# First layer's attention weights: the fifth block of a pair goes to the matrix engine unsplit, in single precision

## What is computed

```
q = (norm(x) @ Wq).reshape(b, s, 32, 16);  k, v = split(norm(x) @ Wkv)    # one k and v of 16 columns for all 32 heads
scores = q k^T / 4 + slope_h * (key position - query position), causal
out = softmax(scores) @ v;  x = x + norm(out @ Wo)
```

## Time and profile before

| | us |
|---|---|
| median of the timed runs | 2204.15 |
| time of the profiled execution | 2197.44 |
| span of its trace | 2195.3 |
| steps with the 64 pairs, about | 100 to 586 |
| PE busy over the span | 2057.3 |
| DVE busy over the span | 1755.9 |
| POOL busy over the span | 937.6 |

### The profile page before, as it was taken

One profiled execution on the slowest core, in us unless ns is written; L12 is line 12 of the kernel. 1 busy time (PEld: TensorE's weight loads), 2 busy tenths in 40 slices (PEclk: granted clock), 3 DMA queues, 4 the chain that ended last, 5 costly groups with the idle time before them and its releaser, 6 DMA issues. The chain is left out here.

```text
span 2195.3 us, 48564 instructions
## 1 busy us (share of the span) xinstructions
PE 2057.3 (94%) x18563; PEld 1244.2 (57%) x18563; DVE 1755.9 (80%) x3692; ACT 1389.0 (63%) x3037; POOL 937.6 (43%) x902
## 2 busy tenths in 40 slices
PE   8788989898868999999999999999999999888998
PEld 3466666566434556666566666666666666534443
DVE  5799998998766787878878788777877887977665
ACT  3466665666456777777777777767777776661221
POOL 0278787879743223333333332333323323253221
PEclk9999999999889999999999999999999999999999
DMA  6110101101122463454345445344344444420001
GB/s 241 47 36 17 55 17 47 36 18 41 44 96 55 87 102 70 78 101 87 67 92 90 73 89 92 66 97 91 62 96 86 73 83 83 98 71 29 29 20 39
DMA packets 390214, 153.81 MB, mean 70 GB/s; under 512 B 358544, under 2 KB 369424, under 8 KB 387936
## 3 DMA queue, kind: packets, MB, share of 16 engines
q1 hardware_dynamic: 389984, 150.71, 31.6%
HBM read 48.69 MB, written 11.53 MB: 27 GB/s over the span
## 5 line engine op out<-in xcount | busy, mean ns | idle before, releaser
L1899 POOL TENSOR_TENSOR q_in_sbuf<-q_in_sbuf,sinq 128x512 f32<-128x512 f32 x128 | 162.5, 1270 | 718.0 <-ACT q_in_sbuf L2031 598.1
L2043 ACT ACTIVATE xp<-xp,nm 128x128 f32<-128x128 f32 (+3 forms) x512 | 281.3, 550 | 199.0 <-DVE nm L2126 199.0
L1925 PE MATMUL bank<-xT_hi,weights_and_hi 128*128 128x512 f16 x1280 | 382.5, 381 | 5.3 <-PEq L103 3.2
L872 ACT ACTIVATE weights_and_hi<-bank,unit 128x512 f32<-128x512 f32 x320 | 213.2, 686 | 166.4 <-PE bank L671 160.5
L2008 ACT ACTIVATE probs_hi<-xp,rl 128x128 f16<-128x128 f32 (+3 forms) x512 | 245.1, 550 | 67.3 <-DVE rl L2146 64.4
L2095 DVE SCALAR_TENSOR_TENSOR probs_lo<-xp,rl,probs_hi 128x128 f16<-128x128 f32 (+3 forms) x512 | 282.3, 611 | 0.0
L2103 DVE TENSOR_TENSOR q1T_lo<-qf,q1T_hi 128x512 f16<-128x512 f32 x128 | 88.4, 690 | 220.6 <-ACT q1T_hi L2022 220.6
L2126 DVE CUSTOM_DVE_ANT_0 xp<-bank,mask,cs 128x128 f32<-128x128 f32 (+3 forms) x512 | 250.2, 544 | 0.0
L1925 PE MATMUL bank<-xT_lo,weights_and_hi 128*128 128x512 f16 x640 | 243.6, 381 | 0.0
L564 POOL CAST weights_and_hi<-weights_and_hi 128x1024 f16<-128x1024 f32 (+1 forms) x192 | 187.7, 996 | 104.0 <-ACT weights_and_hi L872 103.7
L1925 PE MATMUL bank<-p1T_hi,v_hi 128*128 128x128 f16 x1280 | 221.4, 219 | 2.6 <-DMA p1T_lo<-probs_lo 2.6
(11 more groups left out here) (311 smaller groups left out, 5472.3 us busy)
## 6 DMA issues: line engine op xcount, KB each, us to landing
weights_and_hi<-in_wq SPq DMA_DIRECT2D x8, 1024.0 KB, 5.8
raw_o<-in_wo SPq DMA_DIRECT2D x8, 1024.0 KB, 6.1
x_front<-in_x SPq DMA_DIRECT2D x5, 1024.0 KB, 6.1
q_stack<-q_hi SPq DMA_DIRECT2D x64, 64.0 KB, 2.6
wup<-in_wup SPq DMA_DIRECT2D x3, 1024.0 KB, 11.9
fused_scratch<-weights_and_hi SPq DMA_DIRECT2D x12, 256.0 KB, 2.6
xb<-in_x SPq DMA_DIRECT2D x3, 1024.0 KB, 5.4
x_scratch<-xb SPq DMA_DIRECT2D x3, 1024.0 KB, 4.8
```

Of the source, the lines that this page charges most:

```text
L872: act.activation(px[:, p % 2, i, :], bank_of(("x", p, i))[:, :], ACT.Exp, scale=unit[:, 0:1]).then_inc(s_ed, 1)
L1899: pool.tensor_tensor(qs[:, i % 2, :], qs[:, i % 2, :], rope["sink" if u[0] == "k" else "sinq"][:, :], ALU.mult).then_inc(s_rot, 1)
L1925: ins = pe.matmul(out, lhs(a), rhs(c), start=(first and i == 0), stop=(last and i == 2))
L2043: ins = act.activation(x, x, ACT.Exp, scale=-1.0, bias=nm[:, m % 3, t:t + 1], accum_out=ls[:, m % 3, t:t + 1])
```

## The change

The fifth block of a pair is neither rounded nor subtracted any more. `weigh_values` takes it from `px` as it is, float32, and multiplies it with the values in float32 (`vf`, a new copy of the values with its column of ones): one matmul call where there were three. ACT writes `vf` by a second copy out of PSUM, and PE and DVE wait for that copy. The semaphore of POOL's subtraction goes. PE waits for ACT's exponential of the block instead, ACT waits for the product of the pair two before where it waited for that subtraction, and SP's wait for the last subtraction goes.

```
-        ph = [N1.ph, sc.sb("weights_lo", [P, 2, 5, S], F16)]
+        vf = sc.sb("v_full", [P, 2, TT, EV])
+        ph = [N1.ph, sc.sb("weights_lo", [P, 2, 4, S], F16)]
...
                     if n == NP + V_LAG:
                         sp.wait_ge(s_wl, 2 * NP)
-                        sp.wait_ge(s_wc, NP)
                         N1.load_q(sp)
...
+                pool.memset(vf[:, :, :, E0:EV], 1.0)
...
                 def weights_hi(p):
                     if p >= 2:
                         pool.wait_ge(s_pf, p - 1)
-                    for i, (c0, c1) in enumerate(((0, 2), (2, 4), (4, 5))):
+                    for c0, c1 in ((0, 2), (2, 4)):
                         pool.wait_ge(*emptied[("x", p, c1 - 1)])
                         pool.tensor_copy(ph[0][:, p % 2, c0:c1, :], px[:, p % 2, c0:c1, :]).then_inc(s_wh, 1)
-                    pool.wait_ge(s_wh, 3 * p + 3)
-                    pool.tensor_tensor(ph[1][:, p % 2, 4, :], px[:, p % 2, 4, :], ph[0][:, p % 2, 4, :],
-                                       ALU.subtract).then_inc(s_wc, 1)
...
                     if p % PAIRS == 0:
                         pe.wait_ge(s_vd, p // PAIRS + 1)
+                        pe.wait_ge(s_vn, p // PAIRS + 1)
                     pe.wait_ge(s_wl, 2 * p + 2)
-                    pe.wait_ge(s_wc, p + 1)
+                    pe.wait_ge(*emptied[("x", p, 4)])
...
                                 i, c = block_of(e, j, t)
+                                if i == 4:
+                                    ins = pe.matmul(out[:, at:at + EV], px[:, p % 2, i, c:c + P], vf[:, p // PAIRS % 2, j, :],
+                                                    start=False, stop=(j == t), skip_group_check=True)
+                                    continue
...
+                        act.activation(vf[:, b % 2, :, 0:E0],
+                                       bank_of(u)[:, 0:TT * E0].rearrange("p (t e) -> p t e", e=E0),
+                                       ACT.Copy).then_inc(s_vn, 1)
...
-                        act.wait_ge(*((s_wl, 2 * (p - 2) + 1), (s_wl, 2 * (p - 2) + 2), (s_wc, p - 1))[i // 2])
+                        act.wait_ge(*((s_wl, 2 * (p - 2) + 1), (s_wl, 2 * (p - 2) + 2), (s_pf, p - 1))[i // 2])
...
                         dve.wait_ge(s_vh, b + 1)
+                        dve.wait_ge(s_vn, b + 1)
...
-                    dve.wait_ge(s_wh, 3 * p + i + 1)
+                    dve.wait_ge(s_wh, 2 * p + i + 1)
```

More of the change, by code:

```diff
@@ L319, in layer0 @@
         s_wl = sc.sem("s_weights_lo")
-        s_wc = sc.sem("s_last_weights_lo")
+        s_vn = sc.sem("s_values_in_full")
         s_vh = sc.sem("s_values_hi")
```

## The result

The change makes the kernel slightly slower: median 2209.06 us (20 runs) against 2202.86 us (20 runs of the kernel before on the same chip), ratio 1.003, 95% interval 1.0022 to 1.0039, so +6.2 us. The forecast was +2.5 us, and 2206.5 us on the median of 2204.15 that the first three runs had given. The profiled execution took 2205.74 us with a span of 2203.7; before it was 2197.44 and 2195.3.

The account below looks back on a forecast made before the run. DVE was taken to bound plain steps, PE often product steps, POOL late ones. Main steps +6, coupling +1, copy +0.5, late -5 gave +2.5: 2206.5 us on the 2204.15 median; range 2193 to 2229, the forecast's own 2200 to 2210.

Parts of the forecast that it names:

- within 0.2%: Whole kernel: the forecast's own case, near +2.5 us, 0.2% being 4.4 us; chance 0.38.
- Slower by over 0.2%: Whole kernel: cases 1 and 2, the same as rival 1 (with four passes) and Rival 2; chance 0.37.
- What bounds the kernel: Main steps: DVE bounds steps without a product, PE often those with one; larger sums give 420 of 423.5 us.
- Two passes of 0.11 us a call, +0.58 a pair: PE's float32 product: 0.22 us a call, 0.88 a pair, less 0.30 for 12 float16 matmuls, net +0.58 us.
- rival 1: Float32 passes on PE take 182 ns each: +28 in main steps, -3 late, +25 us, 2229; chance 0.17.
- case of four passes with a load each: Float32 calls on PE take the skill page's four passes: +41 - 3, 2242 us; chance 0.05.
- 14 us relief of DVE: Main steps: 14 of 21 us that DVE's subtractions lose go, those behind POOL's removed subtraction.
- Main steps +6 and +1 for coupling: 55 steps: larger of PE and DVE sums to 426 against 420 us, +6; short waits between them add +1.
- The copy, +0.5: ACT's `vf` copy, 0.21 us four times, with DVE and the bank waiting for it: at most +0.5 us.
- Late steps -5: From 537 us, where POOL sets the pace from 542: its removed work gives -5 us, bounds -1 and -10.
- Rival 2: DVE's steps don't hide PE's time: nearly all 32 us show, less 14 and 5; +13, 2217 us; chance 0.15.
- Rival 3: POOL's freed time clears DVE's other 7 us: -8, 2196 us; sign, subtractions under 1.25 us; chance 0.25 with cheap passes.

Follow-up runs that it names:

- pe_half: Kernel before with the 4 float32 calls a pair in place of the 12 float16 matmuls, POOL's cast and subtraction kept; ratio 1.011, 2226.2 us.
- early_signal: Changed kernel with the 48 float16 matmuls first, raising their own semaphore for POOL and DVE, then the float32 calls; 1.0031 to the kernel before, 2209.31 us.
- pool_half: Changed kernel with 12 float16 matmuls a pair again for the float32 calls, POOL's cast and subtraction still gone; 0.9881 to the kernel before, 2176.24 us.
- values_copy: Kernel before plus only the copy `vf`, its memset and its waits, no float32 call; ratio 1.000, 2201.36 us.
- late_pairs: Kernel before with single precision, without POOL's work, for the last 10 pairs only; ratio 0.9998, 2201.88 us.
- deferred: Kernel before with POOL's subtraction of the fifth block moved behind the first cast of the next pair; ratio 1.0004, 2201.93 us.
- calls_twice: Changed kernel with each float32 call issued twice; ratio 1.0432 to the kernel before, 2297.07 us.

## Why the prediction was right in kind and short in size

The forecast was +2.5 us, its own range 2200 to 2210. 2209.06 lies in it, but the effect is +6.2 us (4.8 to 8.6 by the interval), over the 4.4 us that I had called no change, so the case with the largest chance, "within 0.2%", did not come. "Slower by over 0.2%" had 0.37, for cases 1 and 2, and neither is what made it slower. The absolute number flatters the forecast: it stood on the median of three runs, 1.3 us above that of 20, so it looks 2.6 us off where the effect is 3.7 off. Point by point:

- **What bounds the kernel.** Right: plain steps are DVE's, product steps PE's. In pe_half 23 plain steps hid all but 0.8 us of 23 x 0.58; in the changed kernel the growth stands in the product steps.
- **Two passes of 0.11 us a call, +0.58 a pair.** Right to the hundredth: 0.22 us a call, group 2.10. With it rival 1 falls. So does the case of four passes with a load each, which "FP8 and Floating Point Precision", section TensorE Precision Notes, of the Trainium skill made me weigh: 512 loads and matmuls for 256 calls, at 0.22 us a call. Whether each of the two is two passes inside, no run here shows.
- **14 us relief of DVE.** As a term of this change about right (398.8 to 386.8, -12), as a model of POOL a little small: alone, POOL's half frees 18.5. The other 6.5 us don't appear in the changed kernel because POOL's first cast now waits for PE's longer product and falls on DVE again (10.4 us; early_signal, in which that wait is 0.3 us, has DVE busy for 381.6, and pool_half with 0.7 for 380.3), and they would buy little, as early_signal shows.
- **Main steps +6 and +1 for coupling.** Forecast +7.5 with the copy, measured +9.8 and +8.4 in two profiles. By kind: product steps +11.5 where the account had +10.0, plain steps -2.0 and -3.4 where it had -4.7. One plain step at half clock, 6.20 us before and 8.70 after, is 2.5 us of that. How the account pairs a step of DVE with a step of PE matters for its base and less for its change: from the trace of before, five ways of pairing give 413 to 423 us and +3.5 to +7.9. So +6 stands, while "holds within 1%" and the +1 that was taken from that shortfall hang on the pairing. That the main steps cost more than forecast is within what two profiles can differ by (values_copy, 2.5 us), so it is not shown.
- **The copy, +0.5.** Nothing measurable (1.000).
- **Late steps -5.** This is the term that failed. The first profile shows -5.0, the second -0.3, and late_pairs, which has this part alone, -1.1 and a ratio of 0.9998. The step as I put it, "1.7 us less in two steps and 1.0 in the third, where PE at its half clock then needs about 6.6", took PE's half clock to hold in one step of three. One step of the three, 8.41 us in the earlier trace rows, in the kernel before and in the two profiles of the changed one:

```profile
555.39:563.80 8.41, 5.22 (x76) 3.11 (x77) 5.58 (x10) 2.81 (x5) 8.33 (x8) 0.50 0.01 2
563.21:568.27 5.06, 4.15 (x74) 3.17 (x73) 4.22 (x10) 3.25 (x7) 4.79 (x8) 1.00 0.00 0
563.63:570.47 6.84, 6.45 (x74) 4.62 (x73) 5.14 (x11) 3.39 (x8) 5.13 (x7) 0.50 0.00 1
```

POOL was busy nearly all the time before (8.33 of 8.41 us); without its work the step takes 5.06 us at full clock and 6.84, with PE busy for 6.45, at half. Over the eight late steps of the second profile PE is busy 45.14 of 48.26 us at a clock of 0.72 and POOL only 29.97. In eight profiles, of the seven kernels here whose last ten pairs are in single precision with each call issued once and POOL's work gone, the late steps take 43.5 us at a clock of 0.88, 46.3 at 0.82, 45.5 at 0.81, 47.3 and 47.4 at 0.78, and 48.0, 48.3 and 48.3 at 0.72. Their mean is 46.8 us, 1.7 less than before: my own lower bound, "-1, if PE's half clock takes most of it", was much the better value. With -1 the sum is +6.5 us, against +6.2 measured; that it comes so close is partly luck, since the main steps were short by 1 to 2 us. That the late stage was below full clock most of the time stood in the earlier trace rows (0.65).
- **Rival 2, +13.** Wrong while POOL's work stays (in pe_half the plain steps hide PE's time but for 0.8 us), and partly right once it is gone: from pool_half to early_signal 6 of the 13 us show there.
- **Rival 3, -8.** The mechanism exists, but is small: 2.4 of the 7 us go in pool_half. Its sign, a mean under about 1.25 us, doesn't decide: pool_half has 1.279 and gains 26 us, early_signal has 1.272 and gains nothing.

Why the halves miss their sum by 9 us is only in part shown. 18.5 - 12 = 6.5 us of DVE's relief are not there when both are in, and early_signal, which has nearly all of them back, gives 1.5 to 3 us of plain steps and no time of the kernel that can be measured. The larger part, some 5 us, is PE's time showing in plain steps once DVE is relieved (6 us from pool_half to early_signal, 0.8 in pe_half). Whether there PE is the larger in more steps or short waits go back and forth was not taken apart.

Why the step at 204 us falls to half clock in the changed kernel, in both profiles, and not before, is open too. In the step ahead PE had idled 1.5 us of 7.04 and 1.2 of 6.78; in early_signal, with the same work on PE, it idled 1.0 of 6.55, and the clock stayed full. But before, PE idled 1.2 us of 6.21 there at full clock throughout. So in these profiles it goes with the later release of the buffers; how, no run shows.

## What to carry to other kernels

When two engines take turns as the bound, moving work from the helper of one (POOL beside DVE) to the other (PE) is priced step by step, by the larger of the two sums in each step, and neither half alone tells the result: here -26 and +23 gave +6. That price is a first one: the account had +5.3 us for the 54 steps (9.5 and 8.1 measured in two profiles), and it saw only 2 of the 9 us that were lost in the combination. In a stretch whose granted clock is well below 1, take the time that PE would need at that clock as the new bound before booking any gain of another engine. Before paying 0.58 us of a nearly full engine for relief of another, look for a way that costs it nothing, and price what waits for the moved work: here the cheap move (deferred) only handed the wait from DVE to PE.

## What the runs showed of the hardware

- A float32 call with 128 stationary and 17 moving columns is two loads and two matmuls, 0.22 us in a stream, where the three float16 matmuls in its place take 0.076. "TensorE: Matmul & The Clock Gate", section Weight-path perf modes, of the Trainium skill says that the fast way of loading weights is not for FP32. The trace agrees in kind: 0.11 us for a float32 load and matmul, 25 ns for a float16 one.
- A subtraction of two tensors in SBUF takes either its own time or that and the rest of the other engine's instruction, on either side: DVE's 1.16 or 2.04 us behind POOL's, POOL's 1.16 or 2.14 behind DVE's in deferred. "SBUF — State Buffer", section Who interferes with whom, of the Trainium skill says that a DVE instruction with two SBUF inputs contends with a GpSimd instruction that reads SBUF. The runs agree, and show the cost in a tuned loop: in the main steps 108 us of removed POOL work (340.9 to 232.8) were worth 18.5 us of DVE's busy time.
- PE can be busy 98% of a stretch and still run below full clock: 499.9 of 510 us busy, granted clock 0.91, in calls_twice. Its groups of 17-column matmuls last 3.0 us where the changed kernel's last 2.1; what brings the clock down was not taken apart.
